# Value matmuls two steps behind the scores, and diagonal steps in couples, in a causal attention layer on one core

## What is computed

```python
x = x + attn(layernorm(x), Wq, Wk, Wv, Wo)       # rope on Q and K
x = x + relu(layernorm(x) @ w1 + b1) @ w2 + b2
# attn, for each batch and head:
scores = Q @ K.T / 4, with -inf above the diagonal
out = softmax(scores) @ V, then @ Wo
```

## Time and profile before

| | us |
|---|---|
| median of three executions | 2092.21 |
| the profiled execution | 2093.28 |
| its span, first to last instruction | 2091.50 |
| TensorE matmul busy | 1944.1 |
| VectorE busy | 1874.4 |
| ScalarE busy | 1473.9 |
| GpSimd busy | 636.9 |

### The profile page before, as it was taken

The page is one execution under the profiler, slowest core; times in us unless marked ns, Lnnn a source line. Parts: engine busy times, 40 slices in busy tenths (PEclk is TensorE's granted clock), DMA queues, the critical chain, the costliest instruction groups (busy, mean ns, idle before and its releaser), DMA issues. The chain is left out here.

```text
span 2091.5 us, 53450 instructions
## 1 busy us (share of the span) xinstructions
PE 1944.1 (93%) x19104; PEld 781.3 (37%) x19104; DVE 1874.4 (90%) x4039; ACT 1473.9 (70%) x3092; POOL 636.9 (30%) x1265
## 2 busy tenths in 40 slices
PE   5787499999999999999999999999999879999998
PEld 3444022222222222222232222222222246777776
DVE  7999799999999999999999999999999157777775
ACT  5665078888888888888888888888888823323232
POOL 7999522121222212222122221222212323333331
PEclk9999589999999999999999999999999989999999
DMA  5666530321303213042230322304210212222220
GB/s 174 225 207 216 162 62 23 79 42 44 69 23 79 41 45 69 23 79 40 47 69 23 79 37 49 69 23 79 40 37 19 72 57 86 86 86 81 82 83 26
DMA packets 133319, 153.17 MB, mean 73 GB/s; under 512 B 23904, under 2 KB 99424, under 8 KB 132832
## 3 DMA queue, kind: packets, MB, share of 16 engines
q1 hardware_dynamic: 133088, 150.19, 27.6%
HBM read 90.38 MB, written 59.77 MB: 72 GB/s over the span
## 5 line engine op out<-in xcount | busy, mean ns | idle before, releaser
L879 ACT ACTIVATE s_prob<-s_ps 128x512 f32<-128x512 f32 (+3 forms) x2560 | 1198.3, 537 | 177.3 <-PE s_ps L722 145.1
L807 DVE TENSOR_REDUCE s_part<-s_ps 128x2 f32<-128x1024 f32 x768 | 875.1, 1219 | 7.4 <-PE s_ps L705 7.1
L741 PE MATMUL s_ps<-s_prob,s_v 128*32 128x256 f32 (+3 forms) x10240 | 736.6, 359 | 14.8 <-ACT s_o L870 12.1
L705 PE MATMUL s_ps<-mk,mq 64*128 64x512 f16 (+3 forms) x2560 | 680.6, 356 | 52.4 <-DVE s_part L807 21.2
L722 PE MATMUL s_ps<-aq,ak 64*128 64x512 f16 (+3 forms) x2560 | 714.1, 351 | 5.2 <-ACT s_prob L879 2.3
L909 POOL TENSOR_SCALAR_AFFINE_SELECT s_prob<-s_prob 128x128 f32<-128x128 f32 x1024 | 286.5, 292 | 1089.0 <-ACT s_prob L879 1071.4
L814 DVE CUSTOM_DVE_ANT_0 s_ps<-s_ps,mask_sb 128x512 f32<-128x512 f32 (+3 forms) x1024 | 463.3, 538 | 2.8 <-PE s_ps L705 1.9
L741 PEld LDWEIGHTS s_ps<-s_prob,s_v 128*32 128x32 f32 x10240 | 201.9, 108 | 433.9 <-issue 213.5
L722 PEld LDWEIGHTS s_ps<-aq,ak 64*128 64x128 f16 x2560 | 176.1, 93 | 489.6 <-ACT s_prob L879 459.1
L705 PEld LDWEIGHTS s_ps<-mk,mq 64*128 64x128 f16 x2560 | 166.2, 93 | 124.1 <-DVE s_part L807 50.7
L1177 ACT ACTIVATE s_h_f<-s_ps,s_b_s 128x512 f32<-128x512 f32 x128 | 87.9, 687 | 107.4 <-PE s_ps L1042 86.4
(11 more groups left out here) (88 smaller groups left out, 1581.3 us busy)
## 6 DMA issues: line engine op xcount, KB each, us to landing
v_scratch<-s_vst SPq DMA_DIRECT2D x32, 512.0 KB, 4.0
s_v<-v_scratch SPq DMA_DIRECT2D x16, 1024.0 KB, 11.6
att_scratch<-s_o SPq DMA_DIRECT2D x64, 256.0 KB, 2.4
aq<-qk_scratch SPq DMA_DIRECT2D x96, 128.0 KB, 4.4
ak<-qk_scratch SPq DMA_DIRECT2D x96, 128.0 KB, 7.0
s_xin<-x SPq DMA_DIRECT2D x16, 512.0 KB, 4.4
qk_scratch<-s_r_lo SPq DMA_DIRECT2D x64, 128.0 KB, 2.2
qk_scratch<-s_r_hi SPq DMA_DIRECT2D x64, 128.0 KB, 2.3
```

The source lines that it names most:

```text
L705: nc.tensor.matmul(ps[:, bank_of(use + jj), 0:w], mq[rows, p, pair, qt * P:(qt + 1) * P], mk[rows, p, pair, kc * CH:kc * CH + w], start=Tr ...
L741: last = nc.tensor.matmul(ps[32 * j:32 * j + 32, O_BANK, cols], v[:, p, kb, j, :], prob[:, s % 2, j, cols], start=kb == 0 and part == 0, s ...
L807: nc.vector.tensor_reduce(part[:, qt // TPC, :, pair, qt % TPC, kc], ps[:, bank_of(use):bank_of(use) + 2, 0:w], AX.X, ALU.max).then_inc(m_ ...
L879: nc.scalar.activation(prob[:, s % 2, j, q0:CH], ps[:, s_bank(s, j), q0:CH], ACT.Exp, scale=1.0 / (SQK * DK ** 0.5)).then_inc(p_done, 1)
```

## The change

- `prob` gets three buffers instead of two (NPROB = 3), chosen by (40i + s) mod 3. `pv_done` is preset to 3.
- `value_step` runs the values of step s-2 (BEHIND = 2) instead of s-1; behind the last iteration two value steps are left instead of one.
- `copy_o` comes behind the exponentials of the second step after a chunk's last, instead of the first (s = 1 of the next iteration for chunk 3).
- Diagonal steps that have a maximum tile get the order score 0, maximum 1, value half, score 1, maximum 0, score 2, maximum 1, value half, score 3, maximum 0.
- Maximum pairs run heads 1, 0 everywhere, and VectorE reads them in that order; a maximum waits for its own bank's reading.

```diff
+        NPROB = 3
-        prob = sb("s2_prob", [P, 2, G, CH], F32)
+        prob = sb("s2_prob", [P, NPROB, G, CH], F32)
+        BEHIND = NPROB - 1
+        def prob_of(i, s):
+            return prob[:, (NS * i + s) % NPROB]
...
-            def max_pair(t, pair, heads=(0, 1)):
+            def max_pair(t, pair, heads=(1, 0)):
...
-                    if crosses_diagonal(qt, kc):
-                        pe.wait_ge(m_read, use + jj + 1)
-                    elif jj == heads[0]:
-                        pe.wait_ge(m_read, use + 2)
+                    pe.wait_ge(m_read, use + 2 - jj)
...
-                if s > 0:
-                    pv_step(i, p, s - 1, part)
+                if s >= BEHIND:
+                    pv_step(i, p, s - BEHIND, part)
                 elif i > 0:
-                    pv_step(i - 1, 1 - p, NS - 1, part)
+                    pv_step(i - 1, 1 - p, NS + s - BEHIND, part)
...
+                    if t < STEPS_M:
+
+                        score_tile(i, p, s, 0)
+                        max_pair(t, 0, (1,))
+                        value_step(i, p, s, 0)
+                        score_tile(i, p, s, 1)
+                        max_pair(t, 0, (0,))
+                        score_tile(i, p, s, 2)
+                        max_pair(t, 1, (1,))
+                        value_step(i, p, s, 1)
+                        score_tile(i, p, s, 3)
+                        max_pair(t, 1, (0,))
+                        continue
                     score_tile(i, p, s, 0)
                     score_tile(i, p, s, 1)
-                    if t < STEPS_M:
-                        max_pair(t, 0)
-                    elif is_diagonal(s):
+                    if is_diagonal(s):
                         filler_pair(p, s, 0)
...
-            pv_step(NIT - 1, 1, NS - 1, 0)
-            pv_step(NIT - 1, 1, NS - 1, 1)
+            for s in range(NS - BEHIND, NS):
+                for part in range(2):
+                    pv_step(NIT - 1, 1, s, part)
...
-                for jj in range(2):
+                for jj in (1, 0):
                     bank = bank_of(use + jj)
-                    dve.wait_ge(m_ready, use + jj + 1)
+                    dve.wait_ge(m_ready, use + 2 - jj)
...
-                act.wait_ge(pv_done, NS * i + CHUNK_END[c] + 1 + 2)
+                act.wait_ge(pv_done, NS * i + CHUNK_END[c] + 1 + NPROB)
...
-                    if s == 0 and not first:
+                    if s == BEHIND - 1 and not first:
                         copy_o(i - 1, NC - 1)
                     for cc in range(NC):
-                        if cc != LATE and s == CHUNK_END[cc] + 1:
+                        if cc != LATE and s == CHUNK_END[cc] + BEHIND:
                             copy_o(i, cc)
```

More of the change, by code:

```diff
@@ L741, in pv_step @@
                     last = nc.tensor.matmul(ps[32 * j:32 * j + 32, O_BANK, cols], v[:, p, kb, j, :],
-                                            prob[:, s % 2, j, cols], start=kb == 0 and part == 0,
+                                            prob_of(i, s)[:, j, cols], start=kb == 0 and part == 0,
                                             stop=kb == TPC * (c + 1) - 1 and part == 1)
@@ L782, in iteration @@
                     score_tile(i, p, s, 3)
-                    if t < STEPS_M:
-                        max_pair(t, 1)
-                    elif is_diagonal(s):
+                    if is_diagonal(s):
                         filler_pair(p, s, 1)
@@ L878, in iteration @@
                         act.wait_ge(s_ready, ST * i + G * s + j + 1)
-                        nc.scalar.activation(prob[:, s % 2, j, q0:CH], ps[:, s_bank(s, j), q0:CH], ACT.Exp,
+                        nc.scalar.activation(prob_of(i, s)[:, j, q0:CH], ps[:, s_bank(s, j), q0:CH], ACT.Exp,
                                              scale=1.0 / (SQK * DK ** 0.5)).then_inc(p_done, 1)
-                    if s == 0 and not first:
+                    if s == BEHIND - 1 and not first:
                         copy_o(i - 1, NC - 1)
                     for cc in range(NC):
-                        if cc != LATE and s == CHUNK_END[cc] + 1:
+                        if cc != LATE and s == CHUNK_END[cc] + BEHIND:
                             copy_o(i, cc)
@@ L898, in _ @@
         def _(pool):
-            pool.sem_inc(pv_done, 2)
+            pool.sem_inc(pv_done, NPROB)
             def mask_step(i, s):
@@ L905, in mask_step @@
                 for j in range(G):
-                    block = prob[:, s % 2, j, q0:q0 + P]
+                    block = prob_of(i, s)[:, j, q0:q0 + P]
                     pool.wait_ge(p_done, ST * i + G * s + j + 1 + G)
```

## The result

| | us |
|---|---|
| kernel before, median of 20 executions | 2091.94 (2088.59 to 2093.89) |
| changed kernel, median of 20 | 2095.78 (2090.48 to 2105.92) |
| ratio | 1.0024, 95% interval 1.0016 to 1.0032 |
| profiled execution of the changed kernel, span | 2096.03 (before: 2091.51) |

The change costs 0.24% by the ratio; the two medians alone stand 0.18% apart. I had forecast a gain of 0.36% and a range that ends at 2092.5. The sign was wrong, though the difference lies within the 0.3% that I called no change.

What follows compares the result with a forecast made beforehand. VectorE was taken to bound the iterations. Gains of 16 x (0.40 + 0.24) = 10.2 us less losses of 1.6 and 1.0 gave 7.6 us, so a forecast of 2084.6 us, range 2080.5 to 2092.5.

Steps and rivals of the forecast that it cites:

- What bounds the kernel: Attention stage: VectorE sets the pace from 280 to 1626 us; TensorE improvements are worth only VectorE's waiting.
- the sum over the diagonal steps: A chunk's four diagonal steps: TensorE would take 7.28 us instead of 7.87, against VectorE's 7.13.
- lead of 0.40: Full steps: TensorE's matmuls end 0.40 us before VectorE starts on them; no larger because the four maximum banks are full.
- the first wait: VectorE's wait behind chunk 1's last diagonal step, s = 11: would go, worth 0.40 us per iteration, bounds 0.33 and 0.48.
- My check: Chunk 1's diagonal steps in the kernel before: VectorE's lateness computed as 0.34 us, against 0.33 idle in the trace.
- The second wait: VectorE's wait three reductions after chunk 1's diagonal steps: would go with the later output copy, 0.24 us, bounds 0 and 0.25.
- The copy across the boundary: Chunk 3's copy, moved to s = 1: TensorE waits 0.7 us at s = 2; VectorE loses 0.1, bounds 0 and 0.3.
- The rows for chunk 1: Loads queued behind the moved store, needed at s = 4: would land in time, no cost, bounds 0 and 0.7 us.
- rival 2: Rows of chunk 1 land after 717.2, TensorE stands still at s = 4: slower, 2095.8 or 2100 us; chance 0.10.
- The tail: After the last maximum at 1626: wider values and two value steps left cost 1.0 us, bounds 0.5 and 2.
- Rival 1: Stalls only move: copy wait late in the third full step, s = 2 costs its upper bound; about 2092 us, chance 0.13.
- Rival 3: Diagonal steps stay about 7.6 us, scores waiting for exponentials; the second wait stays; 2089.5 us, chance 0.12.

Runs made afterwards that it cites:

- e5: Changed kernel with values of the two widest diagonal steps 128 columns narrower in chunks 1 to 3 (left out); 2089.89 us, ratio 0.9985.
- e4: Changed kernel with the full steps' order in diagonal steps too, both maxima of a pair ahead of the value half; 2093.39 us, ratio 1.0001.
- e2: Changed kernel with diagonal steps back in the old order, values still two steps behind, three buffers; 2100.01 us, ratio 1.0026.
- e1: Changed kernel where the next chunk 0's values do not wait for chunk 3's copy, which reads o_sb (outputs left out); 2091.78 us, ratio 0.9990.
- e8: Changed kernel with chunk 3's copy ahead of the last exponential of s = 1 instead of behind it; 2089.66 us, ratio 0.9990.
- e11: e8 with the second value half of each chunk's last diagonal step behind the next step's first maxima, four probability buffers; 2086.54 us, ratio 0.9975.
- e9: e8 with a pair of filler matmuls in every full step of the last 20 steps too; 2088.93 us, ratio 0.9979.
- e12: e11 with the fillers of e9; 2086.54 us, ratio 0.9969.
- e3: Changed kernel with values one step behind and two buffers, keeping its new diagonal order; 2269.53 us, ratio 1.0854.
- e6: e4's order, with the values catching up at each chunk's end so the output copy comes where it was before; 2106.72 us, ratio 1.0067.
- e10: Kernel before, with the same fillers as e9 in the full steps of the last 20; 2092.22 us, ratio 1.0003.
- e7: Changed kernel, its diagonal order kept, with the values catching up at each chunk's end as in e6; 2097.86 us, ratio 1.0026.

## Why the prediction was wrong

**What bounds the kernel** was read rightly: within the iterations every experiment moved the time by what VectorE waited, or by the clock.

**The step that failed first is the sum over the diagonal steps.** I set the four steps together (7.28 against 7.13) against a lead of 0.40, and concluded that the first wait goes and nothing is lost elsewhere. Measured: 0.27 gained at s = 11 where I had 0.40, and 0.10, 0.05 and about 0.1 lost in the D3 of the three other chunks where I had nothing. That is 16 x 0.38 = 6 us, the largest error. Three things in the working were wrong.
- The lead. I took 0.40 from the end of the maxima to VectorE's start as all slack. But the kernel before shows what the signal itself takes. F0's maxima, in a row of before that I had not set beside the earlier trace rows, end at 733.75 + 0.60 = 734.35 (a modelled end), and VectorE starts at 734.50, waiting for nothing else, 0.15 later. By this the lead was 0.25, not 0.40.

```profile
733.75 0.60 PE L705 MATMUL s_ps<-mk,mq 64*128 64x512 f16 x2
```
 My check (0.34 against 0.33 idle) came out right by comparing with the idle time; against the 0.48 between starts it would have shown the 0.15.
- The sum over four steps. 7.28 against 7.13 lets TensorE keep what it saves in D0 and D1. It cannot, because the four maximum banks are full; what counts is D2 and D3 alone, where by my own pieces TensorE needs 1.76 + 1.36 = 3.12 and VectorE 2.52. I had the rule of the full banks in the text, two parts earlier, and did not apply it. The lag makes just these steps heavier (2.87 before by the same pieces): e5 shows it. The changed kernel took 7.64 us for chunk 1's four steps, from the first score of D0 to that of F0, not 7.28:

```profile
725.90 0.39 PE L724 MATMUL s_ps<-aq,ak 64*128 64x512 f16 x1
...
733.54 0.59 PE L724 MATMUL s_ps<-aq,ak 64*128 64x512 f16 x2
```

- Averages over a step. VectorE takes diagonal tiles head by head, and in couples the second head stands behind a value half. The worst head decides, not the step's total (e4 against e2 and the changed kernel).

**The second wait** went, as forecast, for 0.24.

**The copy across the boundary** is the second term that was mis-sized. TensorE's wait was forecast at 0.7, and its idle time was 0.46 (start to start 0.74). What VectorE makes of it was put at 0.1 with 0.3 as upper bound, and is 0.31 to 0.33: e1 and e8 show it by taking the wait away in two ways. That is 16 x 0.22 = 3.5 us. That it is the same missing 0.15 to 0.2 of the signal at each head is my reading, and no run separates it.

**The rows for chunk 1** (rival 2) are not it: TensorE waited for them once, 0.4 us, though they were issued 1.64 us later than before (713.91, have 712.27). In e1, where TensorE comes sooner, it met that wait 12 times at its weight loads, without a loss in VectorE's starts. The Trainium skill's fixed cost of about 2.0 us ("DMA: Bandwidth & Descriptors", Anatomy of one DMA), given there for the GpSimd path while SyncE issues these, and counted from the end of the issue as I had done, would as an estimate have put them at 713.91 + 1.14 + 2.0 = 717.05. TensorE began F0 at about 716.5 in this iteration without a wait, so here they had landed sooner.

**The tail**: forecast +1.0, measured 46.5 against 44.7 with a fall of the clock of 3.4 us in it, 45.3 to 45.5 in e11, e9 and e12 without one: +0.7, right.

**The clock** is what I left out altogether: I took TensorE's times as fixed. Of the sixteen falls before the tail in all these profiles but e3's, twelve are at s = 1 or 2 by VectorE's step, within the only eight diagonal steps in a row (s = 36 to 39 and 0 to 3), and others come at the start of the tail. By the 20 executions it is about 1.5 us per 0.001 of mean clock, and it makes at least half of the measured 3.8 us.

The Trainium skill ("TensorE: Matmul & The Clock Gate", Part 1) describes a gate that passes half the clock when the engine has been less busy and says it is activity that opens it. The rows above fit it as far as they go: half the clock after 3.38 busy of 4 us with the wait at s = 2 in them, full clock in e9's tail with its fillers. But e11's tail held full clock without those fillers.

Rival 1 (the stalls only move) came nearest, at 2092, with the wrong place for one of them: F2 was never late. Rival 3's sign, diagonal steps over 7.5 us long, came true (7.64 in chunk 1), but its reason, scores waiting for exponentials, shows in TensorE's waits at s = 0 alone, and its other half, that the second wait stays, did not.

**Left open.** Why a fall comes in some executions and not in others, and why at s = 1 in iterations 11 to 13 and not in all fifteen, which have the same wait. That the falls at s = 1 come from the copy's wait is supported by e1, e2, e8, e9, e11 and e12, in which TensorE does not lose 0.46 us to it and which have none there, and by e5, which keeps it and has one. Against it stand e4 and e6, which are without that loss and have two and six there. TensorE's waits as a whole do not sort the runs either: 300 to 1620 us they are 16.5 us in e6, with six falls, and 25.4 us in the kernel before, with none. One profile of each is a small sample. In the tail the profiles with fillers in the full steps (e9, e10, e12) have no fall, but those of the kernel before, e3, e5, e7 and e11 have none either.

## What to carry to other kernels

When the bounding engine takes its work in small pieces through few banks, a producer's average over a phase says nothing: walk the narrowest pieces one by one, with the banks' limit and the signal's own time between the end of the one and the start of the other. Moving work to later steps also moves it beside other work; look at what is smallest there. And before moving matmuls or waits around on a TensorE that is only just busy enough, look at whether the granted clock holds. Removing the wait at s = 2 was worth the most here (0.0034 in the ratio, e8); filler matmuls added little to the median (0.0011 or less) but took away the slow executions.

## What the runs showed of the hardware

- From the end of the last matmul of a tile to VectorE's start on it: 0.15 us for a reduction (734.35 to 734.50 in the kernel before; the matmul's end is modelled).
- The granted clock can fall for 3 us in the middle of a stage in which TensorE is busy 97 us of 100 by the profile; it cost 1.2 to 1.6 us of an 87 us iteration, and in the tail up to 34 us at half clock and 12 us of time.
- The falls can repeat exactly one iteration, 88.8 us, apart (five in a row in e6, three in the changed kernel).
- 24 more filler matmuls in the last 20 steps did not move the kernel before (e10); the spread of e8's twelve executions was 17 us, that of the eleven of e9, which has them, 5, and that of e11 and e12 10 and 3.
